# A post-norm transformer layer on eight cores: half of the weight-statistics loads and half of the reload of v are issued from ScalarE's queue instead of SyncE's

## The chip, the cores and the metric

The kernel runs on the 8 cores of one Trainium2 chip. Each core takes one of the 8 sequences (2048 tokens, 2048 features) through the whole layer, with its own copies of the weights; the cores exchange nothing. The metric is the device time in microseconds of the slowest core.

## What is computed

```python
# attention over FEATURES (2048 x 2048 scores), per sequence
q = x @ Wq ; k = x @ Wk ; v = x @ Wv                     # [s, f]
scores = (q.T @ k) / sqrt(64)                            # [e, f], sum over s
out = (softmax(scores, -1) @ v.T).T @ Wo
x = layernorm(x + out)

def absmean_quant(w):                                    # ternary weights
    scale = mean(abs(w))                                 # over the whole matrix
    return sign(w) * (abs(w) >= scale * 0.7)
h = gelu(x @ absmean_quant(w1).T + b1)                   # w1 [8192, 2048]
x = layernorm(x + h @ absmean_quant(w2).T + b2)          # w2 [2048, 8192]
```

The threshold of the quantiser needs the mean of |w| over all 16.8 million elements of w1, and of w2, before the first element can be quantised. So both matrices are read twice.

## The kernel before, in words

The program is a row of blocks (p1, p2, p3, p4, f1, f2). At the end of a block all engines meet before the next begins. All DMAs that SP and ACT issue go through `DStream.issue` (L54), so in the profile they all have line L58; POOL's too. SP issues on queue q1, ACT on q10, POOL on q0.

**p1 (L243 to L446)** does two things at once.

- The projections on PE. x_fm (16 MB, cast to bf16 by the load) stays in `big0`. POOL loads four 512-column chunks of wq and then four of wk into the two halves of `wbuf` (L260 to L268), a chunk's load waiting until the chunk two before it has been computed. A chunk gives 16 PSUM tiles of 16 matmuls (L298). DVE copies the q tiles into `spillb` (L344) and the k tiles into `big1` (L350). Each four q tiles are one "spill": ACT issues its store to `q_h` (`q_spill`, L386), and DVE may write the next but one group only when the spill that used the same half of `spillb` has landed (L343). Then come 16 V tiles of 64 matmuls each (L313). For each, ACT casts a 1 MB slice of wv from `qin` into `wbuf` (`v_cast`, L408), issues the load of the next slice, and issues the store of the previous V tile to `v_h` (L418).
- The statistics. 256 tiles of 128 x 1024 f32 (512 KB) of w1t and w2t go into three buffers, `sbin`. SP issues the load of tile i when the activation of tile i - 3 is over (L279). ACT sums the absolute values of each tile (L429).

ACT does all of this in one fixed order: activation i, then what is due at i. Spill number h is issued at i = 8(h + 1). The V casts 0 to 11 are at i = 176 + 4f; the casts 12 to 15 come after the last statistics tile. Casts and spills make ACT wait for PE and DVE where these are behind.

**p2 (L452 to L594)** computes 16 row blocks of scores from q, reloaded slice by slice, and k in `big1`. DVE takes the maximum and ACT the exponential (L589). DVE also quantises 24 of the weight tiles there, POOL loads these and SP spills them. After the last of these spills SP waits until `v_h` is written and PE is done (t_s = 16), and issues the four 2 MB loads of v into `big1` (L474).

**p3 (L601 to L664)** transposes a block of the exponentials on PE (L621), ACT copies it out (L656), and PE multiplies it with v (L633); the first of these waits for all four loads of v (L628). DVE quantises on, and so it does in p4 (output projection and layer norm) and f1 (first FFN matmul). f2 is the second FFN matmul and the last layer norm. The change touches none of these.

Of the kernel before, what the change touches and what calls it, by code (L numbers as in the profile page):

```python
# [11 lines left out]
P = 128  # L12
S = 2048
# [3 lines left out]
nE = E // P  # L17
# [13 lines left out]
N_QT = 256  # L31
# [16 lines left out]
class DStream:  # L48
# [5 lines left out]
    def issue(self, eng, out, in_):  # L54
        i = self.n
        self.n += 1
        s = self.sems[i % len(self.sems)]
        eng.dma_start(out=out, in_=in_).then_inc(s.h, 16)  # L58
        s.inc(16)
        return i  # L60
# [18 lines left out]
def build_nc(upto=6, debug=False):  # L79
# [20 lines left out]
    v_h = nc.dram_tensor("v_h", [E, S], BF16, kind=scratch_kind)  # L100
# [5 lines left out]
    def hap(t, off, dims):  # L106
        return bass.AP(t, off, dims)

    with contextlib.ExitStack() as stx:
# [50 lines left out]
        def w_tile_src(i):  # L160
            if i < 128:
                d_k, jj = i // 8, i % 8
                return hap(w1t, d_k * P * FF + jj * 1024, [[FF, P], [1, 1024]])
            j = i - 128
            f_k, jj = j // 2, j % 2
            return hap(w2t, f_k * P * E + jj * 1024, [[E, P], [1, 1024]])
# [9 lines left out]
        with nc.sbuf_tensor("big0", [P, nE * S], BF16) as big0, \  # L176
# [64 lines left out]
            with nc.sbuf_tensor("big1", [P, nE * S], BF16) as big1:  # L241

                with nc.psum_tensor("psA", [P, 2048], F32) as psA, \  # L243
# [30 lines left out]

                    @blk.sync
                    def _(sy):
                        for i in range(N_QT):
                            if i >= 3:
                                sy.wait_ge(a_st.h, i - 2)  # L279
                            s_stats.issue(  # L280
                                sy, sbin[:, (i % 3) * 1024:(i % 3) * 1024 + 1024],
                                w_tile_src(i))
                        s_misc.issue(sy, b1tmp[:], hap(b1, 0, [[P, nF], [1, P]]))

                    @blk.tensor
# [99 lines left out]
                    def _(s):  # L385
# [12 lines left out]
                        for hidx in range(16):  # L398
# [2 lines left out]
                            spill_at.setdefault(thr, []).append(hidx)  # L401
                        s_wv.issue(s, qin[:, 0:2048],
                                   hap(wv, 0, [[E, P], [P * E, nE], [1, P]]))

                        def v_cast(f_m):
                            s_wv.wait_item(s, f_m)
# [17 lines left out]
                        for i in range(N_QT):  # L424
                            s_stats.wait_item(s, i)
                            if i >= 2:
                                s.wait_ge(a_st.h, i - 1)
                            sink = qmask if i % 2 == 0 else qmask2
                            s.activation(sink[:],  # L429
                                         sbin[:, (i % 3) * 1024:(i % 3) * 1024 + 1024],  # L430
                                         AF.Abs, accum_out=stats_acc[:, i:i + 1]
                                         ).then_inc(a_st.h, 1)
                            a_st.inc(1)
                            for hidx in spill_at.get(i, []):
                                q_spill(hidx)
                            if i in cast_at and cast_at[i] < nE - 4:
                                v_cast(cast_at[i])
# [10 lines left out]
                if upto >= 2:  # L448
                    with nc.psum_tensor("psS0", [P, 2048], F32) as psS0, \
# [10 lines left out]
                        @blk.sync  # L460
                        def _(sy):
                            c_q.wait_all(sy)
                            c_v.wait_first_n(sy, nE)
                            for e in range(nE):
                                if e >= 2:
                                    sy.wait_ge(t_s.h, e - 1)
                                s_qsl.issue(
                                    sy, qsl[:, (e % 2) * 2048:(e % 2) * 2048 + 2048],
                                    hap(q_h, e * P, [[E, P], [P * E, nS], [1, P]]))
                                emit_quant_spills(sy, (e * QT_P2) // nE)  # L470
                            emit_quant_spills(sy, QT_P2)
                            c_v.wait_all(sy)
                            sy.wait_ge(t_s.h, 16)
                            for j in range(4):  # L474
                                s_vre.issue(
                                    sy, big1[:, j * 4 * S:(j + 1) * 4 * S],
                                    hap(v_h, j * 4 * P * S,
                                        [[S, P], [P * S, 4], [1, S]]))
# [103 lines left out]
                        @blk.scalar  # L582
                        def _(s):
                            for e in range(nE):
                                s.wait_ge(v_rm.h, e + 1)
                                if e >= 2:
                                    s.wait_ge(v_rc.h, e - 1)
                                ps = psS0 if e % 2 == 0 else psS1
                                s.activation(big0[:, e * S:e * S + S], ps[:], AF.Exp,  # L589
                                             bias=nmax8[:, e % 2:e % 2 + 1],  # L590
                                             scale=0.125,
                                             accum_out=rsum[:, e % 2:e % 2 + 1]
                                             ).then_inc(a_exp.h, 1)
                                a_exp.inc(1)  # L594

                if upto >= 3:
                    with nc.psum_tensor("psO", [P, 2048], F32) as psO, \
# [565 lines left out]
```

## Time and profile before

| | us |
|---|---|
| median of 2 runs | 3856.13 (3853.87 to 3858.38) |
| the profiled execution | 3852.12 |
| its span, slowest core (core 4) | 3850.6 |
| spans of the 8 cores | 3798.8 to 3850.6 |
| PE busy / DVE / ACT | 3215.0 / 1256.1 / 736.7 |

The profile is of one execution, on core 4. A row of the timeline gives the start and the duration in microseconds, the engine, the line, the operation with its output and input, a count, and in brackets the idle time of the engine before it and what ended that. `SPq` and `ACTq` are the issues of DMAs by SP's and ACT's sequencers: how long the sequencer is held, not how long the transfer takes. The DMA share is the mean busy share of the core's 16 DMA engines. Each statistics tile gives ACT two instructions, the activation and the read of its accumulator.

### The profile page before, as it was taken

How to read it: one execution, taken by the hardware profiler on the slowest of the kernel's cores; microseconds unless marked ns; L12 is line 12 of the kernel's file. 1: busy time of each engine (PE TensorE's matmuls, PEld its weight loads, DVE VectorE, ACT ScalarE, POOL GpSimd, SP SyncE). 2: the span in 40 equal slices, each digit the busy share in tenths (PEclk: the TensorE clock that was granted, in tenths of full speed). 3: DMA queues.
4: the chain of work that ended last, by engine and by line, in shares of the span. 5: the costliest groups of instructions: out<-in, count | busy, mean ns of one | idle time of the engine just before them, and what ended most of it. 6: DMA issues, size and time to landing. Idle time of an engine off the chain costs nothing. (4 is left out here: it accounts for less than half of the span.)

```text
span 3850.6 us, 37262 instructions; the slowest of 8 cores (3798.8 to 3850.6 us)
## 1 busy us (share of the span) xinstructions
PE 3215.0 (83%) x14622; PEld 1456.0 (38%) x14917; DVE 1256.1 (33%) x1362; ACT 736.7 (19%) x1065; POOL 92.6 (2%) x166
## 2 busy tenths in 40 slices
PE   0987899926985788677759999999988999989997
PEld 0433344412432333233324444444433444434443
DVE  0111211101443444255533333444422333333333
ACT  1344432440111111134321111111110000300003
POOL 0000000000000000000000000000000000000000
PEclk9998999968997999888879999999999999989998
DMA  9899965875345444556557766777757233452232
GB/s 189 216 257 250 250 181 148 247 228 109 98 115 164 141 138 131 149 191 214 196 151 191 191 188 188 186 185 189 203 164 250 74 129 131 162 209 113 85 131 88
DMA packets 357615, 656.84 MB, mean 171 GB/s; under 512 B 177152, under 2 KB 234560, under 8 KB 332864
## 3 DMA queue, kind: packets, MB, share of 16 engines
q1 hardware_dynamic: 258192, 369.16, 30.8%
q0 software_dynamic: 41648, 184.60, 20.3%
q10 hardware_dynamic: 57600, 100.67, 7.4%
q8 instruction: 119, 1.95, 0.2%
q14 instruction: 56, 0.46, 0.0%
HBM read 536.98 MB, written 150.99 MB: 179 GB/s over the span
## 5 line engine op out<-in xcount | busy, mean ns | idle before, releaser
L896 PE MATMUL psH<-big,w1sl 128*128 128x512 bf16 x4014 | 884.5, 380 | 19.6 <-DMA w1sl<-w1q_h 14.8
L990 PE MATMUL psF<-w2g,hg 128*128 128x512 bf16 x4012 | 886.5, 380 | 5.1 <-issue 0.8
L896 PEld LDWEIGHTS psH<-big,w1sl 128*128 128x128 bf16 x4096 | 399.7, 98 | 504.1 <-issue 28.0
L990 PEld LDWEIGHTS psF<-w2g,hg 128*128 128x128 bf16 x4096 | 400.6, 98 | 490.9 <-issue 14.3
L1040 DVE TENSOR_TENSOR oacc<-psF,oacc 128x2048 f32<-128x2048 f32 x112 | 256.6, 2292 | 585.1 <-PE psF L990 585.1
L224 DVE TENSOR_SCALAR qmask<-qin,tbc 128x1024 f32<-128x1024 f32 x256 | 208.0, 813 | 722.2 <-DMA qin<-w2t 452.0
L235 DVE TENSOR_TENSOR qout<-qmask 128x1024 bf16<-128x1024 f32 x256 | 313.8, 1226 | 157.4 <-DMA w2q_h<-qout 68.9
L429 ACT ACTIVATE qmask<-sbin 128x1024 f32<-128x1024 f32 x256 | 270.0, 1055 | 477.7 <-DMA sbin<-w1t 205.8
L298 PE MATMUL psA<-wbuf,big 128*128 128x512 bf16 x1004 | 228.7, 386 | 112.8 <-DMA wbuf<-wq 97.5
L633 PE MATMUL psO<-big,atsl 128*128 128x512 bf16 x1000 | 245.0, 408 | 85.8 <-ACT atsl L656 56.7
L913 ACT ACTIVATE hstg<-psH,b1sb 128x2048 bf16<-128x2048 f32 x64 | 125.9, 1967 | 753.7 <-PE psH L896 753.7
L298 PE MATMUL psB<-wbuf,big 128*128 128x512 bf16 x1004 | 230.4, 388 | 40.5 <-DVE spillb L344 39.2
L496 PE MATMUL psS<-big,qsl 128*128 128x512 bf16 x1003 | 224.8, 383 | 41.6 <-DMA qsl<-q_h 40.6
L227 DVE TENSOR_SCALAR qmask<-qin,tbc 128x1024 f32<-128x1024 f32 x256 | 206.9, 808 | 0.0
L298 PEld LDWEIGHTS psA<-wbuf,big 128*128 128x128 bf16 x1024 | 101.4, 99 | 237.8 <-issue 121.6
L633 PEld LDWEIGHTS psO<-big,atsl 128*128 128x128 bf16 x1024 | 105.0, 104 | 220.8 <-issue 118.1
L313 PE MATMUL psA<-big,wbuf 128*128 128x512 bf16 x501 | 112.8, 383 | 77.4 <-ACT wbuf L408 76.8
L298 PEld LDWEIGHTS psB<-wbuf,big 128*128 128x128 bf16 x1024 | 101.8, 100 | 167.0 <-issue 51.7
L496 PEld LDWEIGHTS psS<-big,qsl 128*128 128x128 bf16 x1024 | 100.2, 99 | 166.0 <-issue 49.8
L734 PE MATMUL psy<-wbuf,big 128*128 128x512 bf16 x498 | 127.6, 418 | 27.1 <-DVE x2t L767 19.7
L734 PE MATMUL psy<-wobuf,big 128*128 128x512 bf16 x503 | 114.0, 382 | 19.1 <-DMA wobuf<-wo 18.4
L313 PE MATMUL psB<-big,wbuf 128*128 128x512 bf16 x502 | 111.3, 379 | 6.0 <-ACT wbuf L408 5.5
(107 smaller groups left out, 1091.3 us busy)
## 6 DMA issues: line engine op xcount, KB each, us to landing
sbin<-w1t SPq DMA_DIRECT2D x128, 512.0 KB, 5.9
sbin<-w2t SPq DMA_DIRECT2D x128, 512.0 KB, 6.0
qin<-w1t POOLq DMA_DIRECT2D x64, 1024.0 KB, 6.2
qin<-w2t POOLq DMA_DIRECT2D x64, 1024.0 KB, 7.4
w2g<-w2q_h SPq DMA_DIRECT2D x16, 4096.0 KB, 14.9
w1q_h<-qout SPq DMA_DIRECT2D x64, 512.0 KB, 6.7
w1sl<-w1q_h SPq DMA_DIRECT2D x64, 512.0 KB, 10.9
w2q_h<-qout SPq DMA_DIRECT2D x64, 512.0 KB, 9.4
```

Source lines behind the costliest of these rows:

```text
L224: v.tensor_scalar(qmask[:], src, tbc[:, 4 * j:4 * j + 1], tbc[:, 4 * j + 1:4 * j + 2], op0=ALU.subtract, op1=ALU.is_ge)
L227: v.tensor_scalar(qmask2[:], src, tbc[:, 4 * j + 2:4 * j + 3], tbc[:, 4 * j + 3:4 * j + 4], op0=ALU.subtract, op1=ALU.is_le).then_inc(g_qm ...
L235: v.tensor_tensor(qout[:, (i % 2) * 1024:(i % 2) * 1024 + 1024], qmask[:], qmask2[:], op=ALU.subtract).then_inc(v_qt.h, 1)
L298: mm = t.matmul(pv, big0[:, e_k * S + s_m * P:e_k * S + s_m * P + P], half[:, e_k * 512:e_k * 512 + 512], start=(e_k == 0), stop=(e_k == n ...
L313: mm = t.matmul(ps[:, sn * 512:sn * 512 + 512], wbuf[:, (f_m % 8) * 2048 + e_k * P: (f_m % 8) * 2048 + e_k * P + P], big0[:, e_k * S + sn ...
L429: s.activation(sink[:], sbin[:, (i % 3) * 1024:(i % 3) * 1024 + 1024], AF.Abs, accum_out=stats_acc[:, i:i + 1]).then_inc(a_st.h, 1)
L496: mm = t.matmul(ps[:, nb * 512:nb * 512 + 512], qsl[:, (e % 2) * 2048 + s_k * P: (e % 2) * 2048 + s_k * P + P], big1[:, s_k * S + nb * 512 ...
L633: mm = t.matmul(psO[:, sn * 512:sn * 512 + 512], atsl[:, f_k * P:f_k * P + P], big1[:, f_k * S + sn * 512: f_k * S + sn * 512 + 512], star ...
L734: mm = t.matmul(psy[(4 * s_m + nb) % 6][:], big0[:, e_k * S + s_m * P:e_k * S + s_m * P + P], wsrc[:, wof + nb * 512:wof + nb * 512 + 512] ...
L896: mm = t.matmul(ps[:, nb * 512:nb * 512 + 512], w1sl[:, (f_m % 2) * 2048 + d_k * P: (f_m % 2) * 2048 + d_k * P + P], big0[:, d_k * S + nb ...
L990: mm = t.matmul(ps[:, nb * 512:nb * 512 + 512], hg[:, slot * 8192 + f_k * 1024 + j * P: slot * 8192 + f_k * 1024 + j * P + P], w2g[:, slot ...
L1040: v.tensor_tensor(oacc[:, j * 2048:j * 2048 + 2048], ps[:], oacc[:, j * 2048:j * 2048 + 2048], op=ALU.add).then_inc(v_fa.h, 1)
```

## The change

The statistics loads are split by parity. SP issues the even tiles only. ACT issues tile 1 ahead of its loop, and after each even activation i it waits for the end of that activation and issues tile i + 3, which is odd, ahead of a spill or a cast that is due at the same i. The buffers, the three semaphores of the stream and the rule "tile i after activation i - 3" stay as they are; `issue_idx` picks the semaphore by the tile's number.

Of the four loads of v at the end of p2, SP keeps the first two. ACT issues the other two after its last exponential, with the same two waits (`v_h` written, PE done), but not behind the spills of the quantised tiles.

```diff
+    def issue_idx(self, eng, out, in_, i):
         s = self.sems[i % len(self.sems)]
         eng.dma_start(out=out, in_=in_).then_inc(s.h, 16)
         s.inc(16)
...
-                        for i in range(N_QT):
+                        for i in range(0, N_QT, 2):
                             if i >= 3:
                                 sy.wait_ge(a_st.h, i - 2)
-                            s_stats.issue(
+                            s_stats.issue_idx(
                                 sy, sbin[:, (i % 3) * 1024:(i % 3) * 1024 + 1024],
-                                w_tile_src(i))
+                                w_tile_src(i), i)
...
+                        s_stats.issue_idx(s, sbin[:, 1024:2048], w_tile_src(1), 1)
...
                             a_st.inc(1)
+                            if (i + 3) % 2 == 1 and i + 3 < N_QT:
+                                s.wait_ge(a_st.h, i + 1)
+                                s_stats.issue_idx(s, sbin[:, ((i + 3) % 3) * 1024:
+                                                          ((i + 3) % 3) * 1024 + 1024],
+                                                  w_tile_src(i + 3), i + 3)
                             for hidx in spill_at.get(i, []):
                                 q_spill(hidx)
...
-                            for j in range(4):
+                            for j in range(2):
                                 s_vre.issue(
...
                                 a_exp.inc(1)
+                                if e == nE - 1:
+                                    c_v.wait_all(s)
+                                    s.wait_ge(t_s.h, 16)
+                                    for j in range(2, 4):
+                                        s_vre.issue(
+                                            s, big1[:, j * 4 * S:(j + 1) * 4 * S],
+                                            hap(v_h, j * 4 * P * S,
+                                                [[S, P], [P * S, 4], [1, S]]))
```

## Rows read from the trace of the kernel before

**Rows 1.** The page's section 2: the span in 40 slices, busy tenths.

```profile
DMA  9899965875345444556557766777757233452232
```

**Rows 2.** Timeline, PE, 0 to 960 us: start, duration, what, [idle before <-releaser].

```profile
97.50 15.37 PE L298 MATMUL psA<-wbuf,big 128*128 128x512 bf16 x63 [97.50 <-DMA wbuf<-wq]
...
398.34 4.85 PE L298 MATMUL psB<-wbuf,big 128*128 128x512 bf16 x11 [13.39 <-DVE spillb L344]
...
858.36 15.52 PE L313 MATMUL psA<-big,wbuf 128*128 128x512 bf16 x63 [68.39 <-ACT wbuf L408]
```

**Rows 3.** Waits, 0 to 900 us: engine, line, waited for: total us, times, longest.

```profile
ACT qmask L429 <- DMA sbin<-w1t: 205.8, 110, 9.0
DVE spillb L344 <- DMA q_h<-spillb: 203.7, 11, 30.5
...
PE psA L313 <- ACT wbuf L408: 76.8, 7, 68.4
...
ACT wbuf L408 <- PE psB L298: 58.0, 1, 58.0
```

**Rows 4.** Windows: from:to length, PE, PEld, DVE, ACT, POOL busy, PEclk, DMA share, GB/s.

```profile
123.00:155.00 32.00, 31.84 (x147) 14.46 (x148) 6.75 (x10) 16.22 (x30) 0.15 (x1) 1.00 0.87 260
155.00:188.00 33.00, 32.84 (x151) 14.96 (x153) 3.27 (x6) 11.36 (x20) 1.00 (x1) 1.00 1.01 235
785.00:857.00 72.00, 4.92 (x23) 2.06 (x21) 2.29 (x1) 37.34 (x65) 0.00 (x0) 0.56 0.78 234
1210.00:1246.00 36.00, 1.86 (x16) 1.62 (x16) 7.06 (x8) 3.15 (x2) 1.06 (x2) 0.50 0.99 313
```

**Rows 5.** DMA issues, 0 to 900 us: count, KB each, median us to landing.

```profile
q_h<-spillb ACTq DMA_DIRECT2D x16, 512.0 KB, 8.3
wbuf<-wk POOLq DMA_DIRECT2D x4, 2048.0 KB, 34.1
```

**Rows 6.** Timeline, POOL, 0 to 960 us.

```profile
498.82 1.14 POOL L58 DMA_DIRECT2D wbuf<-wk  x1 [54.09 <-PE psB L298]
```

**Rows 7.** Timeline, ACT and its queue (ACTq), 100 to 210 us.

```profile
113.74 0.38 ACTq L58 DMA_DIRECT2D q_h<-spillb  x1
...
129.42 1.06 ACT L429 ACTIVATE qmask<-sbin 128x1024 f32<-128x1024 f32 x1 [0.73 <-DMA sbin<-w1t]
129.52 0.37 ACTq L58 DMA_DIRECT2D q_h<-spillb  x1
130.38 0.19 ACT L429 ACTIVATION_READ_ACCUMULATOR qmask<-sbin 128x1 f32 x1
```

**Rows 8.** Timeline, ACT and ACTq, one V step, 650 to 670 us.

```profile
652.86 1.88 ACT L408 CAST wbuf<-qin 128x2048 bf16<-128x2048 f32 x1
654.82 0.37 ACTq L58 DMA_DIRECT2D qin<-wv  x1
656.02 2.89 ACTq L58 DMA_DIRECT2D v_h<-spillb  x1
659.07 1.06 ACT L429 ACTIVATE qmask<-sbin 128x1024 f32<-128x1024 f32 x1 [4.33 <-issue]
...
666.92 1.06 ACT L429 ACTIVATE qmask<-sbin 128x1024 f32<-128x1024 f32 x1 [4.63 <-DMA sbin<-w2t]
...
667.98 1.88 ACT L408 CAST wbuf<-qin 128x2048 bf16<-128x2048 f32 x1
```

**Rows 9.** The tile sbin, 785 to 860 us: count, ns min/median/max; landing us.

```profile
L58 SPq DMA_DIRECT2D sbin<-w2t x29: 327/328/328, 789.4 to 850.0; - x29
...
DMA to landing us min/median/max: 4.1/5.2/6.1
```

**Rows 10.** Timelines of ACT, SP and PE, 1190 to 1320 us.

```profile
1202.88 1.97 ACT L589 ACTIVATE big<-psS,nmax 128x2048 bf16<-128x2048 f32 x1 [12.86 <-DVE recip_all L570]
...
1209.44 6.26 SPq L58 DMA_DIRECT2D big<-v_h  x4
...
1246.32 16.09 PE L633 MATMUL psO<-big,atsl 128*128 128x512 bf16 x63 [28.10 <-DMA big<-v_h]
```

More of the change, by code:

```diff
@@ L56, in issue @@
         self.n += 1
+        s = self.sems[i % len(self.sems)]
+        eng.dma_start(out=out, in_=in_).then_inc(s.h, 16)
+        s.inc(16)
+        return i
+    def issue_idx(self, eng, out, in_, i):
         s = self.sems[i % len(self.sems)]
```

## Prediction

> **What bounds the kernel now.** I read the page first, then the DMA line of its slices, then PE, ACT, SP and DVE in order of time over the first 1320 us, because every edit lies there. The profiled execution took 3852.1 us (span 3850.6); the two timed runs have a median of 3856.1, which is 4.0 higher. In the first slices the 16 DMA engines are 0.8 to 0.9 busy or more [rows 1]; the page's chain of waits ends in PE's FFN matmuls, where no edit is, so anything won or lost early reaches the end only as a shift. What matters is which early stretches hold PE up [rows 2].
>
> PE starts at 97.5 us, when x_fm and the first wq chunk are in. From then to 398.3 PE computes q and the first K groups, and it stalls on PSUM that DVE can't empty: DVE waited 203.7 us for the spills of q to land [rows 3], and the last stall of PE before 398.3 is for DVE [rows 2]. ACT issues a spill only every eighth statistics tile, so this stretch goes at the pace of the statistics loads. From 398.3 to 608.5 PE is the bound and ACT waits for it. From 610 to 790 ACT and PE go in lockstep, one V tile per 15.1 us (cast at 652.86, next cast at 667.98 [rows 8]) against 13.8 us for 64 matmuls (148 in 32 us [rows 4]). Then PE stands for 68.4 us, while ACT works off the remaining statistics tiles before the next cast [rows 2, 3]. Last, PE waits 28.1 us for v to come back [rows 10].
>
> **The change, part by part.** Nothing is added to the work: the same 256 tiles of 512 KB and the same four 2 MB reloads, with half of each on ACT's queue.
>
> *Start.* ACT stops at its first spill (i = 8, issued at 113.7 [rows 7]) until PE has made four tiles. By then the same 12 tiles are loaded before and after, so the bytes that compete with x_fm are the same: 0 us.
>
> *Price of one issue on ACT.* The even activations are followed by a wait for their own end, then an issue. Today a spill is issued 0.10 us after its activation starts, beside it [rows 7]. In future it is 0.97 + 0.19 us for activation and accumulator read, 0.1 for the wait, 0.37 for the issue (as q's spill [rows 7]; SP's own issue takes 0.33 [rows 9]), 0.16 to the next instruction (656.02 + 2.89 to 659.07 [rows 8]): 1.78 us from the start of an activation to the next instruction. It is 1.06 today where a cast follows (666.92 to 667.98 [rows 8]) and at most 1.27 where an activation follows (SP's next issue starts 1.2 us after the activation at 788.2, at 789.4 [rows 9], and the next activation waits for the same end). So 0.72 us before a cast, 0.5 us before an activation. Queued behind it on ACT are the next activation, the spill and the cast; DVE waits for the spill, PE for both.
>
> *Q stretch, 113.7 to 398.3.* Here 52 issues cost 52 x 0.5 = 26 us of ACT time. Of the 128 tiles of w1t, 110 were waited for, 205.8 us in all [rows 3], and that idle time hides most of it. I take 3 us, with bounds 0 and 26. The spill is now behind a 512 KB tile in ACT's queue and some 1.5 us later at the issue. A spill lands in 8.3 us today [rows 5]; the tile ahead of it adds about 3. In steady state ACT's pace decides, so only the last spill that PE waits for counts: +4.5 us (bounds 0 and 8).
> Against this stands the use of the DMA engines. While POOL's weight load is out (34.1 us each, four of them in the stretch [rows 5]) they are full: share 1.01, and 10 tiles in 33 us (ACT's count is two per tile). Otherwise the share is 0.87, with 15 tiles in 32 us [rows 4]. The gap is (284 - 4 x 34) x 0.13 = 19 us. If two queues take more turns than one, the statistics go faster during a load, the load is spread out, and part of that gap is filled. Another part of the last load can be put off: at most 10 us. I take 5 of these 29 us, near the lower end, since three tiles are in flight before and after. Sum: 3 + 4.5 - 5 = +2.5 us.
>
> *K stretch.* PE-bound; at its end ACT waits 58.0 us for PE before the first cast [rows 3], which covers its issues. Without that cover they would cost 24 x 0.5 = 12 us.
>
> *V lockstep.* A step is ACT's own loop: cast, issue of wv, the spill of v that is blocked behind wv's descriptors until 658.9, three ready activations, the wait for the fourth tile (5 us), its activation, cast [rows 8]. The new issue falls between that activation and the cast. The fourth tile is even and stays on SP at the same time, so the wait for it can't absorb the cost. 11 steps x 0.72 = +7.9 us. The bounds: 0, and +24 if the tile ahead of wv also holds up each of the 11 v spills by 1.5 us (their issue already takes 2.89 here).
>
> *Tail, 785 to 857.* 16 issues x 0.5 = 8 us. The DMA share is only 0.78 [rows 4] because three tiles in flight take 5.2 us each to land, plus the activation [rows 9]. ACT is busy for 37.3 of 72 us [rows 4], so most is hidden: +2 us (bounds -5 and +8). Nothing here is short of issue time: SP needs 0.33 us per 2.1 us [rows 9].
> The Trainium skill (DMA: Bandwidth & Descriptors, "Issuing engines are not separate DMA queues") says that issuing from several engines saves only sequencer time. By it the 5 us of gain in the Q stretch would be 0 and the sum 5 us higher; no row of before can show it, since none has two hardware queues on one stream.
>
> *Reload of v.* Today SP issues all four at 1209.44 to 1215.70, after the last quantised pair has been spilled, and the DMA engines stand nearly still from 1200 to 1209. From 1210 to 1246 they are full (0.99 [rows 4, 10]): every microsecond of earlier start counts. The two issues on ACT go out about 0.1 us after the last exp starts (1202.88), as the q spill does [rows 7], so 6.4 us earlier. They move 4 MB in the time in which nothing else runs. The next block starts some 4 us earlier too, with its 1 MB weight load, but that was inside this stretch anyway. -6.4 us, bounds -2 and -9. The following block is PE-bound and passes it on.
>
> Sum: 2.5 + 7.9 + 2 - 6.4 = +6.0 us, so 3858.1 against the profiled execution. Against the median it would be 3862.1; I take the middle of both bases (3854.1), so **3860 us**.
>
> **The rivals.**
> *A: the two queues win share from POOL's.* Twice as many turns for the statistics during the weight loads; they gain three quarters of the 29 us, 22 instead of 5. For it: the 0.13 of idle share, and loads that have time to spare: a K chunk takes 55.2 us (54.09 + 1.14 between two issues [rows 6]) and a load 34.1. Against: only three tiles are in flight, and the queues are often empty. With 3 more from the reload the time is 3860 - 20 = 3840 us. The Trainium skill's "Queues, rings and completion order" (same page) has each DMA engine serve in turn the queues that have work, which is this rival's mechanism.
> *B, the other sign: the weight load comes too late.* The same share is taken, but a K load that takes over 55.2 us holds PE. If it doubled to 68, the two last K chunks would start 13 us late each: +26 us, 3886. It decides once a load takes 1.6 times as long.
> *C: ACT is the bound after all.* The tiles land in groups of three, so the issues stand exposed: +23 in the Q stretch, +6 in the tail, and half of the 16 us on v's spills: 3860 + 37 = 3897 us. For it: 18 of 128 activations wait for nothing [rows 3]. Against: ACT's 37.3 of 72 us.
> *D: the edits to the statistics do nothing.* The lockstep hides its 7.9 us as well and only the reload is seen: 3854 - 6 = 3848 us.
>
> **How the numbers follow.** Forecast 0.52 (own range 3848 to 3876), A 0.18, B 0.08, C 0.12, D 0.10. Rivals A, B, D and the forecast lie within 3836 to 3892; most of C lies above, so some 0.12 is left out. Two per cent, about what a measurement of this kernel can tell from no change, is 77 us, beyond every case: within it 0.96, slower 0.03 (C with B on top), faster 0.01.
>
> **What would show it.** Right: ACT's cast 1.8 us after the start of the activation before it and V steps of 15.8 us; PE's K matmuls resuming at 396 to 405; wk loads of 34 to 45 us; a stall of 68 to 73 us before the thirteenth V tile; v's first loads issued on ACT near 1203 (shifted by what came before), and PE waiting about 26 us for them instead of 28.1, since the block itself begins some 4 us earlier. Wrong: a Q stretch shorter by over 10 us (A), a PE idle row before K that ends in DMA wbuf<-wk (B), no idle time before activations (C), or ACT's v spills blocked for over 4 us each.

## The result, and the profile after

| | before | after |
|---|---|---|
| median of the runs | 3855.5 us (42 runs) | 3868.5 us (43 runs) |
| ratio after / before | | 1.0036 (95% interval 1.0026 to 1.0046) |
| span of the profiled execution, slowest core | 3850.6 | 3862.1 (core 2) |
| spans of the 8 cores | 3798.8 to 3850.6 | 3842.7 to 3862.1 |

The change makes the kernel slower by 14 us (3853 x 0.0036; 10 to 18 by the interval), 0.36%. It was to cost 6. The medians include executions in which one die ran at a lower clock; the ratios here and below compare the others, a kernel with too few of those has none, and of the kernel with blocks of 8 tiles, whose profile is of such an execution, cores 4 to 7 alone are read tile by tile.

The slowest core is not the same one in each execution, so single cores differ by chance. All stages below are therefore means over the eight cores of one profiled execution; rows are shown from core 4, as ahead of the prediction.

```
us, mean over the 8 cores               before   after   difference
start to PE's first matmul                96.7    96.7     0.0
to PE's last stall for q's spills        297.6   309.0   +11.4
to the first V tile (K groups)           211.9   211.6    -0.3
V tiles 0 to 11 with the casts           177.9   188.4   +10.5
PE's stall before the next V tile         68.4    69.4    +1.0
four V tiles, thresholds, first scores    94.1    95.1    +1.0
score matmuls                            245.0   247.1    +2.1
last score matmul to first with v         44.6    41.2    -3.4
from there to the end                   2592.7  2594.3    +1.6
```

The mean spans of these two executions differ by 23.8 us, more than the 14 of the ratio, so a part of the table is chance. So much it tells: the loss is in two places, each of them in the statistics loads, and a part of the gain in the reload came. How far single rows scatter is seen where the code is the same: "to the last stall for q's spills" is 301.3 in a kernel that changes nothing before it (the reload split alone), the V tiles are 177.9 there, exactly as before. Over all kernels of this study that leave a stage as it was, the V tiles spread from 177.4 to 179.5 and the row of the reload from 43.3 to 44.7.

PE in order of time, core 4 after; the answers to [rows 2] and to the PE row of [rows 10]:

```profile
96.65 16.19 PE L304 MATMUL psA<-wbuf,big 128*128 128x512 bf16 x63 [96.65 <-DMA wbuf<-wq]
...
406.42 4.85 PE L304 MATMUL psB<-wbuf,big 128*128 128x512 bf16 x11 [16.46 <-DVE spillb L350]
...
790.48 13.97 PE L319 MATMUL psB<-big,wbuf 128*128 128x512 bf16 x63 [0.94 <-ACT wbuf L415]
874.03 16.61 PE L319 MATMUL psA<-big,wbuf 128*128 128x512 bf16 x63 [69.58 <-ACT wbuf L415]
...
1254.27 15.94 PE L653 MATMUL psO<-big,atsl 128*128 128x512 bf16 x63 [27.86 <-DMA big<-v_h]
```

PE resumes at 406.4 (398.3 before), the twelfth V tile starts at 790.5 (776.0), and the stall behind it is as long as before, 69.6 against 68.4 us.

The waits of core 4, 0 to 900 us, the answers to [rows 3]:

```profile
ACT qmask L436 <- DMA sbin<-w1t: 227.5, 91, 37.7
DVE spillb L350 <- DMA q_h<-spillb: 215.8, 12, 29.5
...
PE psA L319 <- ACT wbuf L415: 74.4, 5, 69.6
...
ACT wbuf L415 <- PE psB L304: 44.9, 1, 44.9
```

ACT waited for 91 tiles of w1t instead of 110, but longer: 227.5 against 205.8 us, of which one wait of 37.7 is the first, where tile 1 stands behind the load of wv in ACT's queue. That one costs nothing, as PE's start shows. The 44.9 us (58.0 before) at the first cast are the cover of the K stretch, 13 us smaller and still enough (61 and 53 us as means over the cores).

DMA issues of core 4, 0 to 900 us, with the median us to landing, the answers to [rows 5] and [rows 9]:

```profile
sbin<-w1t SPq DMA_DIRECT2D x64, 512.0 KB, 6.0
sbin<-w1t ACTq DMA_DIRECT2D x64, 512.0 KB, 6.0
...
q_h<-spillb ACTq DMA_DIRECT2D x16, 512.0 KB, 6.9
wbuf<-wk POOLq DMA_DIRECT2D x4, 2048.0 KB, 32.3
```

Neither the tiles (5.9 before) nor the spill of q (8.3 before) nor POOL's loads (34.1 before) land later. The last is the opposite of what rival A needs: POOL's queue got more, not less. For the spill core 4 exaggerates: as a mean over the cores it lands in 6.8 us instead of 7.4, and in 7.0 to 7.6 in the other kernels that change nothing there.

One V step of ACT after, the answer to [rows 8]; `ACTq L64` is the new issue:

```profile
675.51 1.90 ACT L415 CAST wbuf<-qin 128x2048 bf16<-128x2048 f32 x1 [0.56 <-ACT qmask L436]
677.49 0.39 ACTq L58 DMA_DIRECT2D qin<-wv  x1
679.50 1.68 ACTq L58 DMA_DIRECT2D v_h<-spillb  x1
681.34 1.06 ACT L436 ACTIVATE qmask<-sbin 128x1024 f32<-128x1024 f32 x1 [3.93 <-issue]
...
682.39 1.04 ACT L436 ACTIVATE qmask<-sbin 128x1024 f32<-128x1024 f32 x1
...
683.60 0.33 ACTq L64 DMA_DIRECT2D sbin<-w2t  x1
684.10 1.06 ACT L436 ACTIVATE qmask<-sbin 128x1024 f32<-128x1024 f32 x1 [0.57 <-ACT qmask L436]
...
690.40 1.06 ACT L436 ACTIVATE qmask<-sbin 128x1024 f32<-128x1024 f32 x1 [5.16 <-DMA sbin<-w2t]
...
691.62 0.34 ACTq L64 DMA_DIRECT2D sbin<-w2t  x1
692.11 1.90 ACT L415 CAST wbuf<-qin 128x2048 bf16<-128x2048 f32 x1 [0.56 <-PE psA L319]
```

From cast to cast it is 16.6 us in this step and 15.9 in the mean (15.1 before). Both new issues are seen: at 683.60, between the second and the third ready activation, which starts 2.76 us after the first instead of 2.09, and at 691.62, with the cast 1.71 us after the start of the activation ahead of it instead of 1.06.

The reload of v, ACT and then SP, the answers to [rows 10]:

```profile
1216.37 1.97 ACT L601 ACTIVATE big<-psS,nmax 128x2048 bf16<-128x2048 f32 x1 [12.84 <-DVE recip_all L582]
1216.57 0.94 ACTq L58 DMA_DIRECT2D big<-v_h  x2
```

```profile
1222.91 0.98 SPq L58 DMA_DIRECT2D big<-v_h  x2
```

ACT issues 0.20 us after the start of its last exponential and 6.3 us ahead of SP, as forecast; SP's two issues hold it for 0.98 us instead of 6.26, so the next block starts 4.5 us earlier.

### The profile page after: what moved, and what is told of

The parts are those of the page before. It is cut to its first block and busy times, and to the rows that moved or that the text cites. A ratio compares the mean times of both kernels' runs of the same rounds, so it can differ in the third digit from the quotient of the medians.

```text
span 3862.1 us, 37265 instructions; the slowest of 8 cores (3842.7 to 3862.1 us)
## 1 busy us (share of the span) xinstructions
PE 3226.6 (84%) x14622; PEld 1460.7 (38%) x14917; DVE 1256.2 (33%) x1362; ACT 738.2 (19%) x1065; POOL 92.6 (2%) x166
## 5 line engine op out<-in xcount | busy, mean ns | idle before, releaser
L916 PE MATMUL psH<-big,w1sl 128*128 128x512 bf16 x4014 | 881.6, 380 | 13.3 <-DMA w1sl<-w1q_h 9.1
```

Of the source, the lines that this page charges most:

```text
L916: mm = t.matmul(ps[:, nb * 512:nb * 512 + 512], w1sl[:, (f_m % 2) * 2048 + d_k * P: (f_m % 2) * 2048 + d_k * P + P], big0[:, d_k * S + nb ...
```

## The experiments

Of the V steps, the middle eight of 11 on all 8 cores are averaged (64 steps); "4th landing" is the time from 1.2 us after the first ready activation, when SP issues the fourth tile, to the start of the activation of that tile. "Q span" is the time from the first to the fourteenth spill issue of q, mean over the cores. The part of a step that has no column, from the cast to the first activation behind it, is the step less the last two columns and less 1.2 us.

```
                          Q span  V tiles   V step  act 1 to  wait for  act 4 to  4th
                          us      0-11, us  us      act 3     4th tile  cast      landing
before                    266.5   177.9     15.11   2.09      4.57      1.06      6.52
reload split alone        269.6   177.9     15.04   2.10      4.39      1.06      6.33
wait alone                269.2   180.9     15.35   2.39      4.40      1.35      6.64
wait and tiny DMA         270.7   181.6     15.30   2.78      3.77      1.73      6.39
one tile, ahead of cast   266.1   183.1     15.55   2.10      4.74      1.71      6.69
one tile, middle          267.7   182.3     15.41   2.76      4.24      1.06      6.84
statistics split alone    273.2   187.5     15.98   2.76      4.52      1.71      7.13
the same, issue by cast   275.3   186.2     15.58   2.76      4.34      1.06      6.95
split below 128 only      276.1   179.5     15.24   2.10      4.71      1.06      6.65
after                     279.2   188.4     15.94   2.76      4.51      1.71      7.12
```

### One edit at a time

The reload split alone (all statistics tiles on SP, as before):

```diff
-                            for j in range(4):
+                            for j in range(2):
                                 s_vre.issue(
...
+                                if e == nE - 1:
+                                    c_v.wait_all(s)
+                                    s.wait_ge(t_s.h, 16)
+                                    for j in range(2, 4):
+                                        s_vre.issue(s, ...)
```

> The kernel before with only the reload of v split (loads 3 and 4 on ACT after its last exponential). The theory of the forecast: the stretch from PE's last score matmul to its first matmul with v, 44.6 us as a mean over the cores before and 41.2 after, is again 41 to 42, and the time is 3 to 4 us below the kernel before (ratio 0.999). Rival: the 3.4 us are scatter between two executions; then the stretch is 44 to 45 and the time equal.

Measured: ratio 0.9979 (0.9966 to 0.9992), so 8 us faster (3 to 13). The stretch from the last score matmul to the first one with v is 41.6 us, 3.0 below the kernel before. Ten kernels whose reload is as before have 43.3 to 44.7 us there, so the stretch is shorter by more than its scatter. This edit is a gain, though the stretch itself shows only the lower end of the interval.

The statistics split alone (the diff shown ahead of the prediction without the reload's part):

> The kernel before with only the statistics loads split. If the whole loss comes from here, the time is 15 to 19 us above the kernel before (13 to 14 of the full change, plus 3.4 of the reload), with +11 us until PE's last stall in the K groups and +10 us over the V steps 0 to 11. Rival: the two edits act on each other, or the Q stretch's +11 us is scatter between executions; then it is +5 to +10 us, most of it in the V steps.

Measured: ratio 1.0053 (1.0028 to 1.0079), 20 us slower (11 to 30). V tiles +9.6 us. The whole loss comes from here.

### Is it ACT's time or its queue?

The wait alone: no load is moved.

```diff
                             a_st.inc(1)
+                            if i % 2 == 0 and i + 3 < N_QT:
+                                s.wait_ge(a_st.h, i + 1)
                             for hidx in spill_at.get(i, []):
```

> All loads on SP as in the kernel before; ACT only gets the wait for the end of its own even activations, which stands ahead of the next activation, spill or cast. Theory 'ACT's own time': the wait costs 0.1 to 0.2 us before a cast and delays a spill by 1.2 us, some 0.2 of the 0.72 us, so V steps +2 us in sum and the Q stretch +1 to +2: +3 to +4 us. Rival 'the wait is nearly all of it, the issue nothing': +15 us, as with the loads split. Rival 'the queue is all of it': 0.

Measured: ratio 1.0013 (0.9998 to 1.0028), about 5 us, with an interval that holds 1; V tiles +3.0, Q span within the scatter. Its ACT rows, a fourth activation and the cast behind it:

```profile
680.13 1.06 ACT L429 ACTIVATE qmask<-sbin 128x1024 f32<-128x1024 f32 x1 [4.52 <-DMA sbin<-w2t]
...
681.48 1.90 ACT L408 CAST wbuf<-qin 128x2048 bf16<-128x2048 f32 x1 [0.20 <-ACT qmask L429]
```

The cast comes 1.35 us after the activation instead of 1.06.

The wait and a tiny DMA in the place of the tile's, so that ACT pays for an issue and no tile is on its queue:

```diff
                             a_st.inc(1)
+                            if i % 2 == 0 and i + 3 < N_QT:
+                                s.wait_ge(a_st.h, i + 1)
+                                s_dum.issue(s, dum[16 * (i // 64):16 * (i // 64) + 16,
+                                                   i % 64:i % 64 + 2],
+                                            hap(ident_in, i % 64, [[P, 16], [1, 2]]))
```

> All statistics tiles stay on SP. After each even activation ACT waits for its end and issues a tiny DMA (16 rows of 8 bytes) where the change issues a tile, so it pays the wait and the issue and moves no bytes to its queue. Theory 'ACT's own time is the loss': as with the loads split, +17 us as a mean over the cores, V steps 187 us instead of 178. Rival 'half time, half queue': the V steps' two delays of 0.65 us are seen (step 15.6 to 16.0 instead of 15.1) but the fourth tile lands as before (6.5 us after its issue, not 7.1), the Q stretch stays as before: +6 to +9 us.

It has no ratio; the reading is that of the profile. ACT pays in full: 2.78 and 1.73 us, even a little more than with the tiles. But the V tiles take only 181.6 us, +3.7 of the +9.6:

```profile
660.87 1.06 ACT L430 ACTIVATE qmask<-sbin 128x1024 f32<-128x1024 f32 x1 [2.81 <-DVE spillb L362]
...
661.93 1.04 ACT L430 ACTIVATE qmask<-sbin 128x1024 f32<-128x1024 f32 x1
...
663.14 0.35 ACTq L58 DMA_DIRECT2D dum<-ident_in  x1
663.65 1.06 ACT L430 ACTIVATE qmask<-sbin 128x1024 f32<-128x1024 f32 x1 [0.59 <-ACT qmask L430]
...
668.45 1.06 ACT L430 ACTIVATE qmask<-sbin 128x1024 f32<-128x1024 f32 x1 [3.65 <-DMA sbin<-w2t]
...
669.67 0.35 ACTq L58 DMA_DIRECT2D dum<-ident_in  x1
670.18 1.90 ACT L409 CAST wbuf<-qin 128x2048 bf16<-128x2048 f32 x1 [0.58 <-ACT qmask L430]
```

The third activation is late by 0.7 us (663.65), the fourth is not: the fourth tile has landed 6.4 us after its issue as before, and the wait for it has shrunk (3.77 us in the mean, 4.57 before). That takes care of the issue in the middle. The issue ahead of the cast costs its 0.67 us, but 0.37 of them come back behind the cast: from the cast to the first activation it is 5.97 us instead of 6.34 (means of the same 64 steps). ACT's store of the previous V tile waits there for DVE's copy of that tile, and it starts 1.67 us after the load of wv instead of 2.16. So a step isn't ACT's own loop alone, and ACT's own time costs 0.2 us a step. With the tiles on its queue the same two parts give 0.2 as well (+0.65 at the cast, -0.43 behind it), and the other 0.6 us are the fourth tile, which lands 7.12 us after its issue instead of 6.52. The theory "ACT's own time is the loss" falls, and so does the reason that the forecast gave for its own +7.9. The Q span, 270.7, is 2.3 us above 268.4, the mean of the eight kernels of this study in which ACT issues nothing new below tile 128. The forecast took 3 us for ACT's time there; but the eight spread from 266.1 to 270.9, so the 2.3 can't be told from none.

### The V steps: which of the two tiles

The loads split, but in a V step the issue goes out behind the start of the cast:

```diff
                         def v_cast(f_m, i=None):
...
                             a_wv.inc(1)
+                            if i is not None:
+                                tile_issue(i)        # the wait and the issue of tile i + 3
                             s.wait_ge(a_wv.h, a_wv.v)
```

> The statistics loads split (no split of the reload), but in the V steps ACT issues tile i + 3 behind the start of the cast and ahead of its end, so that the cast no longer waits for it. Theory 'the issue ahead of the cast costs the V steps': they fall back by 8 us (11 x 0.72) to within 3 us of before, and the time is 8 us below the run with the loads split in the old place. Rival 'the tile ahead of wv in ACT's queue costs the V steps': they stay 10 us longer than before, since the tile is still ahead of wv.

Measured: ratio 1.0042 (1.0021 to 1.0062), not to be told from the split in the old place. The cast is back at 1.06 us after the activation, with the issue beside it:

```profile
687.03 1.06 ACT L444 ACTIVATE qmask<-sbin 128x1024 f32<-128x1024 f32 x1 [5.40 <-DMA sbin<-w2t]
...
688.09 1.88 ACT L421 CAST wbuf<-qin 128x2048 bf16<-128x2048 f32 x1
688.26 0.33 ACTq L64 DMA_DIRECT2D sbin<-w2t  x1
```

Yet the V tiles fall only from 187.5 to 186.2. The step is shorter by 0.40 us, not 0.65: the issue of v's store, blocked behind the load of wv, now ends 4.26 us after the issue of wv instead of 3.81. And the first steps of this execution were longer, which leaves 1.3 us for the whole. So the expected 8 us were wrong by a factor of six, and the rival, the tile's place ahead of wv, keeps most of its loss.

From tile 176 on, only the tile that is issued ahead of the cast on ACT, and only the one in the middle:

```diff
                         for i in range(N_QT):               # SP
+                            if i >= 176 and i % 4 == 3:     # the other kernel: == 1
+                                continue                    # left to ACT
...
                             a_st.inc(1)                     # ACT
+                            if i + 3 >= 176 and (i + 3) % 4 == 3 and i + 3 < N_QT:
+                                s.wait_ge(a_st.h, i + 1)
+                                s_stats.issue_idx(s, ...)
```

> From tile 176 on one tile in four is on ACT, the one whose issue stands between the fourth activation and the cast (ahead of the load of wv in ACT's queue); all others are on SP. Theory 'ACT's own time': +0.65 us a step from act to cast, step 15.5 to 15.7, V steps 183 to 185 us. If the tile ahead of wv is what makes the fourth tile land later, its landing is 7.1 us here; if it is the tile beside it, 6.5.

> The other one of the two: from tile 176 on only the tile that is issued between the second and the third activation is on ACT, behind wv and v's spill in ACT's queue. Theory 'it competes with the fourth tile, which it stood behind on SP': the fourth tile lands 7.1 us after its issue and the third activation is 0.67 us later, step 15.5, V steps 182 to 184 us. My forecast's claim (the wait for the fourth tile covers this issue): step 15.1, V steps 178 us.

Measured: 183.1 and 182.3 us, +5.2 and +4.4, which add up to the +9.6 of both; kernels with nothing new in their V steps differ by 2 us among themselves. (The ratio of the second is 1.0029, 1.0014 to 1.0044, or 5 to 17 us, more than its V tiles show; the first has none.) The rows of the second:

```profile
656.62 1.06 ACT L437 ACTIVATE qmask<-sbin 128x1024 f32<-128x1024 f32 x1 [5.24 <-issue]
...
658.88 0.34 ACTq L64 DMA_DIRECT2D sbin<-w2t  x1
659.37 1.06 ACT L437 ACTIVATE qmask<-sbin 128x1024 f32<-128x1024 f32 x1 [0.57 <-ACT qmask L437]
...
665.25 1.06 ACT L437 ACTIVATE qmask<-sbin 128x1024 f32<-128x1024 f32 x1 [4.73 <-DMA sbin<-w2t]
...
666.30 1.88 ACT L416 CAST wbuf<-qin 128x2048 bf16<-128x2048 f32 x1
```

The forecast said that the wait for the fourth tile hides the middle issue. It hides half: the third activation is 0.67 us late, the wait is 0.33 us shorter, and the tile lands 0.3 us later (6.84). With both tiles moved the landing is 0.6 us later (7.13), and then nothing is hidden. With the tile ahead of the cast alone it is 6.69, and that can't be told from no effect: with all tiles on SP the landing is 6.33 to 6.65. What that tile costs alone is ACT's time, 0.65 us at the cast, of which 0.4 come back behind it. So the middle tile slows the fourth once it is in the other queue, and the two together slow it more; what the first does to it by itself stays open. On SP the middle tile stands behind the fourth; the likely reading is that the DMA engines now share their time between the two. That the landing times differ is measured; the sharing inside the engines is argued.

### The Q stretch: two queues land tiles in pairs

Only the odd tiles below 128 on ACT:

> Only the odd tiles below 128, those of w1t, are on ACT; from 128 on all are on SP, the reload is not split. It shows the Q stretch alone. From the profiles: the 14 spills of the Q stretch span 268 us without and 276 us with the split, so +7 us in the time, and the V steps 178 us as before. Rival 'the Q difference is scatter between executions': 0 to +2 us. Rival 'the spill behind the tile': the last spill is 3 us later; but it landed sooner with the split (12.4 against 13.9 us), which speaks against it.

Measured: ratio 1.0027 (1.0011 to 1.0043), 10 us slower (4 to 17). Q span 276.1, V tiles 179.5. The Q part is real: four kernels with the parity split have spans of 273.2 to 279.2 (mean 276.0), the ten without it 266.1 to 270.9.

The same number of issues on ACT, but in blocks: eight tiles on SP, eight on ACT.

```diff
                         for i in range(N_QT):
+                            if i < 128 and (i // 8) % 2 == 1:
+                                continue
...
+                            if i + 3 < 128 and ((i + 3) // 8) % 2 == 1:
+                                s.wait_ge(a_st.h, i + 1)
+                                s_stats.issue_idx(s, ...)
```

> Below tile 128 the loads change queue in blocks of 8 tiles (8 on SP, 8 on ACT), so ACT issues 64 tiles, nearly as many as with the split by parity, but the tiles in flight mostly share one queue. From 128 on all are on SP. Theory 'two queues land the tiles in pairs': hardly any tiles land within 0.6 us of each other (0 to 2 of 100, not 5 to 9), and the 14 spills of the Q stretch span 269 to 272 us as with the tiny DMA (270.7), not 276; the time is +3 to +5 us instead of +10. Rival 'half of the loads behind ACT's own traffic, or ACT's queue as such, is slower': 274 to 277 us, as with the split by parity.

Measured: Q span 270.2 us, and 269.0 over cores 4 to 7, as in the kernels without a split. The ratio 1.0004 (0.9966 to 1.0043) is too wide to decide between 0 and 10 us. Tile by tile, from the issue and landing times of all eight cores (4 to 7 for the blocks) between 120 and 390 us:

```
                        period of   issue to   landing to   landed within    landed before
                        a tile, us  landing    activation   0.6 us of the    ACT was done with
                                    us         us           one ahead        the one ahead
before                  2.63        6.49       0.14          0 of 802          2
wait and tiny DMA       2.65        6.46       0.24          0 of 797         43
blocks of 8             2.64        6.43       0.24          0 of 400         23
split below 128         2.70        6.39       0.44         49 of 780        190
statistics split alone  2.70        6.36       0.44         31 of 790        184
after                   2.71        6.48       0.37         34 of 775        133
```

Three tiles are in flight, so three periods are one loop: from issue to landing, from landing to activation, and the 1.2 us until the tile is summed and its buffer is loaded again. Other kernels without a split have periods of 2.63 to 2.66. With the parity split the tiles land no later, but 4 to 6 in a hundred land together with the one ahead of them, and 17 to 24 in a hundred land while ACT, which needs 1.3 us for one, is still busy with the one ahead. So the tile that has landed waits: 0.37 to 0.44 us instead of 0.14, of which 0.10 are ACT's own time (the tiny DMA). In blocks hardly anything pairs, and the pace is that of before. The waits of core 4 say the same in short, first the split below 128, then the blocks, against 110 waits of 205.8 us before [rows 3]:

```profile
ACT qmask L438 <- DMA sbin<-w1t: 226.5, 80, 37.1
```

```profile
ACT qmask L437 <- DMA sbin<-w1t: 206.6, 97, 12.6
```

80 waits instead of 110, and longer ones (the first of them, 37.1 us, again behind wv). So ACT's queue as such is not slower, and neither is the issue: in the blocks ACT has nearly as many of them as with the parity split. What costs the Q stretch most of its 8 us is that tiles which are used in turn come through two queues at once. Why tiles on two queues close up is not shown.

### The reload: a microsecond earlier is not a microsecond

Windows of core 4 with the reload split alone, the first ten microseconds of ACT's two loads (length, busy times, clock, DMA share, GB/s), and SP's issues:

```profile
1205.00:1210.00 5.00, 0.00 (x0) 0.00 (x0) 4.11 (x6) 0.59 (x2) 0.00 (x0) 0.50 0.82 218
1210.00:1215.00 5.00, 1.87 (x16) 1.63 (x16) 0.00 (x0) 1.28 (x1) 0.53 (x1) 0.50 0.95 248
```

```profile
1210.09 1.03 SPq L58 DMA_DIRECT2D big<-v_h  x2
```

ACT's two loads go out at 1203.7, 6.35 us ahead of SP's. From the first issue to PE's first matmul it takes 38.5 us as a mean over the cores, against 35.2 when all four are issued at once. That is where half of the 6.4 us went. It is tempting to blame the first windows, 218 and 248 GB/s against the 313 of [rows 4]. But 313 is the mean of a whole reload; in the kernel before, the first ten microseconds behind the issue of all four loads look the same:

```profile
1210.70:1215.70 5.00, 0.00 (x0) 0.00 (x0) 0.00 (x0) 0.00 (x0) 0.00 (x0) 0.50 0.96 225
1215.70:1220.70 5.00, 1.86 (x16) 1.62 (x16) 0.00 (x0) 2.39 (x2) 0.53 (x1) 0.50 0.98 253
```

Summed over the eight cores, from the first issue to the last landing of v the DMA engines move the same 11.5 MB in both kernels, at 328 GB/s before and at 301 with the reload split (303 in the full change). The difference is partly in the first 5 us (187 against 273 GB/s, where the kernel before has the last spill under way too), partly between 16 and 31 us after the first issue (292 to 300 against 330 to 354). So two loads alone are not the whole reason, and why the split reload moves slower later on is not settled.

The four loads on SP, ahead of the last spill of the quantised tiles, nothing on ACT:

```diff
-                            emit_quant_spills(sy, QT_P2)
                             c_v.wait_all(sy)
                             sy.wait_ge(t_s.h, 16)
                             for j in range(4):
                                 s_vre.issue(...)
+                            emit_quant_spills(sy, QT_P2)
```

> The kernel before, but SP issues the four loads of v as soon as PE's last score matmul is over, ahead of the last spill of the quantised tiles, on its own queue. All four start 9.4 us earlier. If each microsecond of earlier start counted: PE's first matmul with v 9.4 us earlier, 35.2 us after the last score matmul. By what the split reload showed (6.3 us earlier gave 3 to 3.4): the block after starts with SP's last issue, and v alone moves slower than v beside other loads; 37 to 40 us instead of 44.6, and the time 5 to 7 us below the kernel before. Rival: nothing beyond the split reload's 3 us, since the stretch is bound by the bytes.

```profile
1200.75 5.93 SPq L58 DMA_DIRECT2D big<-v_h  x4
```

```profile
1214.21 1.86 PE L621 MATMUL psTA<-ident_bf,big 128*128 128x128 bf16 x16 [13.54 <-PEq L452]
1233.57 16.09 PE L633 MATMUL psO<-big,atsl 128*128 128x512 bf16 x64 [17.49 <-DMA big<-v_h]
```

```profile
1234.53 1.23 DVE L235 TENSOR_TENSOR qout<-qmask 128x1024 bf16<-128x1024 f32 x1 [7.70 <-DMA w1q_h<-qout]
```

The first matmul with v comes 31.3 us after the last score matmul as a mean over the cores, 13.3 us less than before: twice what was expected, and more than the 9.3 us by which the issues are earlier. The other 4 us come with fewer bytes. The spill of the quantised tiles now stands behind v in SP's queue and lands 23.6 us after its issue instead of 3.5; DVE waits for it (the last row), and POOL's second 1 MB load, which waits for DVE, goes out 36.1 us after the last score matmul instead of 32.2. So on every core one such load instead of two is issued before v has landed, and 9.9 MB instead of 11.5 are moved until then. The time is 0.9977 (0.9942 to 1.0013) of before, an interval that holds 1.

### A version that beats both

The longest stall of the first third, 68 us, and ACT's idle time of 58 us before the first cast, have one cause, the place of the casts in ACT's order. Moved by 28 tiles, alone and together with the reload ahead of the spill:

```diff
-                        cast_at = {min(176 + 4 * f, N_QT - 1): f for f in range(nE)}
+                        cast_at = {min(204 + 4 * f, N_QT - 1): f for f in range(nE)}
```

> All loads on SP as before; only the V casts 0 to 11 move from tiles 176 + 4f to 204 + 4f of ACT's order. ACT now uses the 58 us for which it waited for PE at tile 176, and 28 fewer statistics tiles are left after cast 11. Theory 'the order on ACT bounds this stretch, not the queue': PE's stall before the thirteenth V tile falls from 68 to about 10 us, V starts within 3 us of before, the time is 52 to 60 us lower (ratio 0.985). Rival: ACT reaches tile 204 late, V starts late by as much: 20 to 40 us lower.

> Both of the edits above, none of the change's. They lie in different stretches, so the sum of the two: 57 to 67 us below the kernel before, ratio 0.984. Rival: the later stages take part of it back (the quantised tiles of the next blocks are not ready earlier): less than the sum.

Measured: ratio 0.9868 (0.9826 to 0.9910), 51 us faster, and with both 0.9818 (0.9784 to 0.9852), 70 us faster, median 3782.4 us. ACT's first cast and PE's first and thirteenth V tile of the second, core 4, and PE's first V tile on core 3:

```profile
609.69 1.90 ACT L408 CAST wbuf<-qin 128x2048 bf16<-128x2048 f32 x1 [0.37 <-PE psB L298]
```

```profile
611.73 15.66 PE L313 MATMUL psA<-big,wbuf 128*128 128x512 bf16 x64 [2.13 <-ACT wbuf L408]
...
799.97 15.58 PE L313 MATMUL psA<-big,wbuf 128*128 128x512 bf16 x64 [8.22 <-ACT wbuf L408]
```

```profile
615.45 16.11 PE L313 MATMUL psA<-big,wbuf 128*128 128x512 bf16 x64 [11.85 <-ACT wbuf L408]
```

On core 4 the cast has waited 0.37 us, V starts as before, and the stall before the thirteenth tile is 8.2 us. On the other cores ACT is a little late: PE waits 4.3 to 11.9 us for the first cast there, 7.7 as a mean over the eight (4.6 with the casts alone) instead of 2.1. That is a small part of the rival's effect, and the place of the casts may be a few tiles too far; no run tried another. As a mean over the cores, PE's way from the first V tile to the end of the last takes 240.6 us with the casts alone and 245.3 with both edits, instead of 303.5. The two edits add up to what was expected within the interval (57 to 67 us expected; 57 to 83 measured).

## Why the prediction was right, and which terms were not

Direction and size hold: 3868.5 us lies in the range of 3836 to 3892 and in the forecast's own range of 3848 to 3876, but more than half of the shift of 14 us was not foreseen. The Q stretch was taken 5 us too low, the reload's gain 3 us too high, the V steps 2 us too low; that the V steps' term is this near is luck, since its reason was wrong.

- **Start, 0.** Right: 96.7 us as a mean over the cores in both, although one tile waits 37.7 us behind wv.
- **Price of an issue on ACT.** Right ahead of a cast: 1.71 us after the activation (forecast 1.78), with the tiny DMA 1.73. Between two activations that are ready it is 0.67 us, not 0.5.
- **Q stretch, +2.5.** Mis-sized: +8 us (276.0 against 268.4 for the mean spans), +11 in the profile of after. ACT's time, forecast as 3, measured 2.3 with the tiny DMA, which is within the scatter. The two others are wrong. The spill was to land 3 us later behind a tile; it landed no later (6.8 against 7.4 us, means over the cores). And the statistics were to win 5 us of idle DMA time; they lost about 5, by the pairs. The step that failed is "near the lower end, since three tiles are in flight before and after": its bounds did not include a loss. By the Trainium skill's sentence that the prediction cites (DMA: Bandwidth & Descriptors, "Issuing engines are not separate DMA queues") the gain would have been 0; the runs show a loss.
- **K stretch, 0.** Right: 211.9 and 211.6; ACT's wait for PE shrank from 58.0 to 44.9 us (core 4) and still covers it. The count of issues was too low: from i = 112, where the Q stretch was counted to end, to the first cast at 176 there are 32 (30 from 398.3 us on), not 24.
- **V lockstep, +7.9.** The size is near (+9.6 to +10.5), the reason is not. The issue ahead of the cast was to cost 0.72 us a step that nothing could absorb, and the issue in the middle nothing. The premise "A step is ACT's own loop" failed: v's store waits for DVE's copy, and 0.4 us a step come back there, so both issues together cost 0.2 us a step. The fourth tile's late landing, which the forecast held fixed ("stays on SP at the same time"), is the other 0.6. It is issued at the same time, but does not land at the same time. That they come near the forecast's sum is luck.
- **Tail, +2.** +1.0.
- **Reload, -6.4.** -3.0 to -3.4 in its stretch, inside the bounds of -2 and -9. The issue is 6.3 us earlier; the premise that every microsecond of earlier start counts failed: the same 11.5 MB moved at 301 to 303 GB/s instead of 328.
- **The rivals.** A needed POOL's loads to take longer; the four that POOL issues between 120 and 400 us took 31.1 to 32.9 us as a mean over the cores in four kernels with the split, 34.4 to 34.9 in the ten others. That speaks against B as well. The rule of turns that the prediction cites beside A (the Trainium skill, same page, "Queues, rings and completion order") gives the second queue its turns, but with three tiles in flight the two together did not get more. C's mark, ACT's v spills blocked for over 4 us each, is absent (3.8 us from wv's issue to their end, 4.2 before). Its tiles that land together did appear, but for 4 to 6 in a hundred. D falls by the stages.

Put together, 8 + 10 + 1 - 3.3 gives 16 us, against 14 (10 to 18) measured.

## What to carry to other kernels

Before work is moved off a queue, look whether that queue is short of issue time: here SP needed 0.33 us for a tile every 2.1 to 2.6, and nothing was to be won. This stream of loads, consumed strictly in order with three in flight, did better in one queue; spread over two, some of its members landed in pairs, and the most urgent one landed later. Where an engine works off one fixed order, look first at where it stands idle and where the others wait for it: here moving the casts by 28 places in ACT's order brought 51 us. Issuing the reload ahead of an unrelated spill on the same queue shortened its stretch by 13 us, where splitting it brought 3; the times of the two whole kernels don't tell them apart.

## What the runs showed of the hardware

- A DMA issue on ACT holds its sequencer for 0.33 us (a 512 KB tile, as on SP) to 0.39 (a 1 MB slice of wv); with the wait for the activation ahead of it, the next instruction comes 1.7 us after that activation starts, instead of 1.05.
- Three tiles in flight on two queues landed after the same 6.4 to 6.5 us as on one, but 4 to 6 in a hundred within 0.6 us of their predecessor instead of none, and a load of POOL beside them took 2 to 3 us less of its 34 to 35.
- Four loads of 2 MB issued by SP in a row, with the traffic beside them 11.5 MB, moved at 328 GB/s; with two of the four issued by ACT 6.3 us earlier the same bytes moved at 301. The cause is open.
- A 512 KB spill that SP issued behind four loads of 2 MB landed after 23.6 us; with the loads behind it, after 3.5.
